# Attention scores of two heads in alternating row halves of TensorE, in a graph layer with mixture of experts

## What is computed

```python
scores = jnp.einsum('hnd,hmd->hnm', q2, k2) * scale + mask[None]
attn = jax.nn.softmax(scores, axis=-1)
out = jnp.einsum('hnm,hmd->hnd', attn, v2)
...
return out @ wo.T + bo
```

## Time and profile before

| | |
|---|---|
| median of 3 runs | 1041.15 us (1040.41 to 1043.7) |
| the profiled execution | 1042.34 us, its span 1040.6 us |
| PE busy | 996.6 us, 96% |
| DVE busy | 775.1 us, 74% |
| ACT busy | 635.5 us, 61% |
| POOL busy | 145.0 us, 14% |
| loop of the heads | about 410 to 540 us of the span |
| score matmuls (L1204) | 144, 64 rows x 128 columns of weights, 384 columns |

### The profile page before, as it was taken

How to read it: one execution, slowest core, us unless ns; L and a number is a source line. 1 busy time by engine, 2 the same in 40 slices (tenths; PEclk the granted TensorE clock), 3 DMA queues, 4 the chain that set the end, 5 groups by cost and what they waited for, 6 DMA issues and landing times.

```text
span 1040.6 us, 15023 instructions
## 1 busy us (share of the span) xinstructions
PE 996.6 (96%) x5191; PEld 848.5 (82%) x5227; DVE 775.1 (74%) x1078; ACT 635.5 (61%) x825; POOL 145.0 (14%) x185
## 2 busy tenths in 40 slices
PE   4999999999999999989999899999999999999898
PEld 4898999888889899978788778788787878788675
DVE  7446888867585869767753788888887878788487
ACT  4357777523322133879952667777777787778472
POOL 3003242410001002243320300000000000000013
PEclk9999999999999999989999899999999999999989
DMA  9562342456546763211105499999999999999886
GB/s 313 168 183 83 100 113 70 126 147 173 166 142 182 213 177 117 82 41 42 41 7 201 182 349 381 386 357 371 378 372 374 374 381 359 363 380 385 298 315 232
DMA packets 140508, 237.33 MB, mean 228 GB/s; under 512 B 6908, under 2 KB 48124, under 8 KB 137892
## 3 DMA queue, kind: packets, MB, share of 16 engines
q1 hardware_dynamic: 135780, 225.91, 63.5%
q0 software_dynamic: 1760, 6.37, 1.6%
q10 hardware_dynamic: 2912, 4.34, 1.1%
HBM read 206.56 MB, written 30.03 MB: 227 GB/s over the span
## 4 chain that ended last, share of the span: by engine, by line
PE 78%; DVE 9%; ACT 7%; DMA 3%; issue 2%; SPq 0%; POOL 0%; ACTq 0%; DVEq 0%; POOLq 0%
PE bank L1322 35%; PE bank L971 5%; PE bank L973 5%; PE bank L972 5%; PE bank L985 4%; PE bank L987 4%; PE bank L986 4%; PE bank L1204 2%; DVE wlo L1397 2%; DMA raw<-in_wffn 2%; PE bank L1121 2%; ACT dense L743 2%; PE bank L1048 2%; PE bank L1218 2%; PE bank L1309 1%
## 5 line engine op out<-in xcount | busy, mean ns | idle before, releaser
L1701 DVE TENSOR_TENSOR wlo<-raw,whi 128x2048 fp32r<-128x2048 f32 x72 | 164.6, 2289 | 28.3 <-ACT whi L869 27.9
L869 ACT ACTIVATE a_all<-raw 128x2048 fp32r<-128x2048 f32 x72 | 138.1, 1918 | 52.5 <-DMA raw<-in_wffn 29.0
L869 ACT ACTIVATE whi<-raw 128x2048 fp32r<-128x2048 f32 x72 | 137.9, 1916 | 42.4 <-DMA raw<-in_wffn 23.5
L1397 DVE TENSOR_TENSOR wlo<-raw,whi 128x1024 fp32r<-128x1024 f32 (+1 forms) x72 | 110.4, 1539 | 49.6 <-ACT whi L658 48.4
L658 ACT ACTIVATE whi<-raw 128x1024 fp32r<-128x1024 f32 (+1 forms) x72 | 89.0, 1242 | 90.8 <-PE bank L973 47.7
L1701 DVE TENSOR_TENSOR t_all<-raw,a_all 128x2048 fp32r<-128x2048 f32 x36 | 82.5, 2293 | 40.8 <-ACT a_all L869 40.6
L971 PE MATMUL bank<-a_all,whi 128*128 128x384 f32 x320 | 109.5, 342 | 0.2 <-DVE t_all L1473 0.2
L1322 PE MATMUL bank<-a_all,xg 128*128 128x512 f32 x360 | 106.7, 410 | 1.0 <-DVE t_all L1701 1.0
L973 PE MATMUL bank<-a_all,wlo 128*128 128x384 f32 x320 | 107.2, 335 | 0.0
L972 PE MATMUL bank<-a_all,whi 128*128 128x384 f32 x320 | 107.1, 335 | 0.0
L1322 PE MATMUL bank<-whi,t_all 128*128 128x512 f32 x288 | 100.4, 410 | 0.0
(11 more groups left out here) (276 smaller groups left out, 2041.5 us busy)
## 6 DMA issues: line engine op xcount, KB each, us to landing
raw<-in_wffn SPq DMA_DIRECT2D x144, 512.0 KB
raw<-in_wffn SPq DMA_DIRECT2D x72, 1024.0 KB
raw<-in_wall SPq DMA_DIRECT2D x28, 1024.0 KB
raw<-in_wall SPq DMA_DIRECT2D x32, 512.0 KB
yrows<-zero SPq DMA_DIRECT2D x24, 512.0 KB, 7.0
y_rows<-zero SPq DMA_DIRECT2D x8, 1024.0 KB, 8.7
dense<-yrows SPq DMA_DIRECT2D x8, 512.0 KB, 7.9
y_rows<-dense ACTq DMA_DIRECT2D x16, 256.0 KB, 5.6
```

What stands on the lines that cost most here:

```text
L869: act.activation(hi_ring[u % RAW], raw[:, u % RAW, :], ACT.Copy).then_inc(hi_done, 2)
L1397: dve.tensor_tensor(ring(wlo, k), part(k), ring(whi, k).bitcast(F32), ALU.subtract).then_inc(lo_done, width(k))
L1701: dve.tensor_tensor(lo_ring[u % RAW], raw[:, u % RAW, :], hi_ring[u % RAW].bitcast(F32), ALU.subtract)\
```

## The change

Scores of both heads of a chunk are made together. A chunk has six tiles, numbered i = 2t + (head in the chunk): the even step makes i = 0 to 3 (row tiles 0 and 1 of both heads), the odd step i = 4 and 5 (row tile 2 of both). The matmuls of a pair alternate between partitions 0 to 63 and 64 to 127. Four banks hold scores, `bank[0:4]`; `bank[3]` was one of the two projection banks. So PE waits in step 0 until all four earlier pieces of the projection have left their banks, and from then on every filling product goes to `bank[7]` and waits for the emptying of the one before.

The odd head's first two tiles are ready a step early, the third tile of both heads in the odd step. So there are three probability buffers instead of two (the third in a part of `mo` that is free by then), PE turns row tiles 0 and 1 of both target tiles first and row tile 2 after a wait of its own. DVE empties the filling product first in its step; in odd steps it normalises ahead of the residuals of the transposed tiles, in even steps behind them as before. Of a chunk's six tiles DVE scales i = 0, 1, 4 and ACT i = 2, 3, 5 (before: two and four). In odd steps ACT has its exponentials ahead of `split2_hi`, in even steps at the old place.

The diff, cut to its core (indented less; the emptyings' new bank index and the statistics' columns are left out in part):

```diff
+prob += [moT[:, KT // 2:KT // 2 + NT, :]]
...
-sc_bank = bank[0:3]
+sc_bank = bank[0:4]
...
 proj_bank = [bank[3], bank[7]]
+TILES = 2 * NT
+def sc_tiles(h):
+    return [(2 * (h // 2) + i % 2, i // 2, i) for i in (range(4, TILES) if h % 2 else range(4))]
+def stat(h, kind, i):
+    return 64 + 20 * (h // 2 % 2) + 6 * kind + i
...
-        if j >= 2:
+        if j >= FIRST2:
+            eng.wait_ge(evicted, 4 * KT + j)
+        elif j >= 2:
             eng.wait_ge(evicted, 4 * KT + j - 1)
...
-        return proj_bank[j % 2]
+        return proj_bank[j % 2 if j < FIRST2 else 1]
...
+    def exps(h):
+        c = h // 2
+        for g, t, i in sc_tiles(h):
+            act.wait_ge(sc_done, TILES * c + i + 1)
+            m, u = stat(h, 0, i), stat(h, 1, i)
+            act.activation(prob[g % 3][:, t, :], prob[g % 3][:, t, :], ACT.Exp, scale=-1.0,
+                           bias=small[:, m:m + 1], accum_out=small[:, u:u + 1]).then_inc(exp_done, 1)
...
+        if h < H and h % 2:
+            exps(h)
         if h % 2 == 1 and (h + 1) // 2 < KT:
             split2_hi((h + 1) // 2)
...
+        if h < H and h % 2 == 0:
+            exps(h)
...
-            for t in range(1, NT):
...
-            last.then_inc(prob_act, 1)
+            for g, t, i in sc_tiles(h):
+                if i in (2, 3, 5):
+                    v = stat(h, 2, i)
+                    act.activation(prob[g % 3][:, t, :], prob[g % 3][:, t, :], ACT.Copy, scale=small[:, v:v + 1]).then_inc(prob_act, 1)
...
-            if i >= 2:
-                pe.wait_ge(mixo_added, i - 1)
+            if i >= 1:
+                pe.wait_ge(mixo_added, i)
             else:
                 pe.wait_ge(evicted, 5 * KT)
             pe.wait_ge(mo_lo, 2)
-        ins = wide(OUT + 2 * j, t, proj_bank[i % 2], *mo_s[kh], True, True, range(2 * half, 2 * half + 2))
+        ins = wide(OUT + 2 * j, t, proj_bank[1], *mo_s[kh], True, True, range(2 * half, 2 * half + 2))
...
+            pe.wait_ge(sc_done, NT * H)
             for t in range(NT - 1):
-                pe.wait_ge(sc_done, NT * (H - 1) + t + 1)
...
         if h < H:
-            lo = HD * (h % 2)
-            q, kk = (qk2[lo:lo + HD, m] for m in range(2))
-            pe.wait_ge(qk_lo, 2 * KT + 2 * (h // 2) + 2)
...
-                    pe.wait_ge(sc_done, NT * (h - 1) + t + 1)
+            c = h // 2
+            pe.wait_ge(qk_lo, 2 * KT + 2 * c + 2)
+            if h == 0:
+                pe.wait_ge(evicted, 4 * KT + FIRST2)
+            tiles = sc_tiles(h)
+            for pair in (tiles[j:j + 2] for j in range(0, len(tiles), 2)):
+                i = pair[1][2]
+                if h % 2:
+                    pe.wait_ge(sc_done, TILES * c + 2)
+                elif c >= 1:
+                    pe.wait_ge(sc_done, TILES * c if i == 1 else TILES * (c - 1) + 4)
                 for n, (q_part, k_part) in enumerate(((0, 0), (0, 1), (1, 0))):
-                    last = pe.matmul(sc_bank[t][:, 0:N], q[:, q_part, t * P:(t + 1) * P], kk[:, k_part, :],
-                                     start=(n == 0), stop=(n == 2))
-                last.then_inc(sc_full, 1)
+                    for g, t, i in pair:
+                        r = slice(HD * (g % 2), HD * (g % 2) + HD)
+                        last = pe.matmul(sc_bank[i % 4][:, 0:N], qk2[r, 0, q_part, t * P:(t + 1) * P], qk2[r, 1, k_part, :],
+                                         start=(n == 0), stop=(n == 2))
+                        if n == 2:
+                            last.then_inc(sc_full, 1)
...
-            pe.wait_ge(prob_ready, g + 1)
-            pe.wait_ge(prob_act, g + 1)
-            for mt in range(NT):
-                if mt == NT - 1:
-                    fill(h, 1)
-                    pe.wait_ge(pt_lo, NT * g + 1)
-                for t in range(NT):
-                    last = pe.transpose(pt_bank[mt][:, t * P:(t + 1) * P], prob[g % 2][:, t, mt * P:(mt + 1) * P], ident[:, :])
-                last.then_inc(pt_full, 1)
+            c = g // 2
+            pe.wait_ge(prob_ready, NT * c + 1 + g % 2)
+            pe.wait_ge(prob_act, NT * c + (3 if g % 2 else 1))
+            def turn(mt, tiles):
+                for t in tiles:
+                    last = pe.transpose(pt_bank[mt][:, t * P:(t + 1) * P], prob[g % 3][:, t, mt * P:(mt + 1) * P], ident[:, :])
+                return last
+            for mt in range(NT - 1):
+                turn(mt, range(NT - 1))
+            pe.wait_ge(prob_ready, NT * c + (2 if g % 2 else 3))
+            for mt in range(NT - 1):
+                turn(mt, (NT - 1,)).then_inc(pt_full, 1)
+            fill(h, 1)
+            pe.wait_ge(pt_lo, NT * g + 1)
+            turn(NT - 1, range(NT)).then_inc(pt_full, 1)
...
+    def minima(h, tiles):
+        c = h // 2
+        for g, t, i in tiles:
+            dve.wait_ge(sc_full, TILES * c + i + 1)
...
+            m = stat(h, 0, i)
+            dve.tensor_tensor_reduce(out=prob[g % 3][:, t, :], in0=sc_bank[i % 4][:, 0:N], in1=mask8[:, t, :],
+                                     scale=-SCALE, scalar=3e38, op0=ALU.add, op1=ALU.min,
+                                     accum_out=small[:, m:m + 1]).then_inc(sc_done, 1)
+    def normalise(h):
+        c, first, n = h // 2, 4 * (h % 2), 2 if h % 2 else 4
+        u, v = stat(h, 1, first), stat(h, 2, first)
+        dve.wait_ge(exp_done, TILES * c + first + n)
+        dve.reciprocal(small[:, v:v + n], small[:, u:u + n]).then_inc(inv_ready, 1)
+        dve.wait_ge(inv_ready, h + 1)
+        for g, t, i in sc_tiles(h):
+            if i in (0, 1, 4):
+                v = stat(h, 2, i)
+                dve.tensor_scalar(prob[g % 3][:, t, :], prob[g % 3][:, t, :], small[:, v:v + 1], None, ALU.mult).then_inc(prob_ready, 1)
...
         if 1 <= h <= KT - FIRST2:
             evict2(K2 + FIRST2 + h - 1)
...
-            dve.tensor_tensor(r, proj_bank[i % 2][:, :], r, ALU.add).then_inc(mixo_added, 1)
+            dve.tensor_tensor(r, proj_bank[1][:, :], r, ALU.add).then_inc(mixo_added, 1)
+        tiles = sc_tiles(h) if h < H else []
+        minima(h, tiles[:len(tiles) // 2])
+        if h >= 2:
+            low_p(h - 2, NT - 1)
+        minima(h, tiles[len(tiles) // 2:])
+        if h < H and h % 2:
+            normalise(h)
         for n in ahead(fill_start[h]) if h in fill_start else ():
             lo(n)
         if 1 <= h <= H:
             for t in range(NT - 1):
                 low_p(h - 1, t)
-        if h < H:
-            dve.wait_ge(exp_done, NT * h + NT)
-            dve.reciprocal(small[:, s + 12:s + 12 + NT], small[:, s + 4:s + 4 + NT]).then_inc(inv_ready, 1)
-            dve.wait_ge(inv_ready, h + 1)
-            dve.tensor_scalar(prob[h % 2][:, 0, :], prob[h % 2][:, 0, :], small[:, s + 12:s + 13], None, ALU.mult).then_inc(prob_ready, 1)
+        if h < H and h % 2 == 0:
+            normalise(h)
```

More of the change, by code:

```diff
@@ L854, in _ @@
                     act.wait_ge(inv_ready, h + 1)
-                    for t in range(1, NT):
-                        i = 76 + 16 * (h % 2) + t
-                        last = act.activation(prob[h % 2][:, t, :], prob[h % 2][:, t, :], ACT.Copy, scale=small[:, i:i + 1])
-                    last.then_inc(prob_act, 1)
+                    for g, t, i in sc_tiles(h):
+                        if i in (2, 3, 5):
+                            v = stat(h, 2, i)
+                            act.activation(prob[g % 3][:, t, :], prob[g % 3][:, t, :], ACT.Copy, scale=small[:, v:v + 1]).then_inc(prob_act, 1)
             def x2_copy(c):
@@ L1657, in low_p @@
                 dve.tensor_tensor(probT[:, 1, t, :], pt_bank[t][:, 0:N], probT[:, 0, t, :].bitcast(F32), ALU.subtract).then_inc(pt_lo, 1)
-            for h in range(H + 2):
-                s = 64 + 16 * (h % 2)
-                for t in range(NT):
-                    if t == NT - 1 and h >= 2:
-                        low_p(h - 2, NT - 1)
-                    if h < H:
-                        dve.wait_ge(sc_full, NT * h + t + 1)
-                        dve.tensor_tensor_reduce(out=prob[h % 2][:, t, :], in0=sc_bank[t][:, 0:N], in1=mask8[:, t, :],
-                                                 scale=-SCALE, scalar=3e38, op0=ALU.add, op1=ALU.min,
-                                                 accum_out=small[:, s + t:s + t + 1]).then_inc(sc_done, 1)
+            def minima(h, tiles):
+                c = h // 2
+                for g, t, i in tiles:
+                    dve.wait_ge(sc_full, TILES * c + i + 1)
+                    if g == 2 and t == 0:
+                        dve.wait_ge(mo_lo, 1)
+                    m = stat(h, 0, i)
[12 more added lines that the diff above has]
+                        dve.tensor_scalar(prob[g % 3][:, t, :], prob[g % 3][:, t, :], small[:, v:v + 1], None, ALU.mult).then_inc(prob_ready, 1)
+            for h in range(H + 2):
                 if 1 <= h <= KT - FIRST2:
```

2 lines of the change are left out of this document (removed).

## The result

| | time, median (lowest to highest) | profiled execution | its span | mean clock of it |
|---|---|---|---|---|
| before | 1040.56 us (1038.77 to 1043.7) | 1042.34 | 1040.6 | 0.988 |
| after | 1048.75 us (1045.6 to 1055.87) | 1055.87 | 1054.1 | 0.977 |

Seven runs of each. The ratio is 1.0084, with an interval of 1.0063 to 1.0105: the change makes the kernel 0.84% slower. The forecast was 1051. Where the two differ is itself a finding.

What follows compares the result with a forecast made beforehand. It took PE as the bound by a small margin over ACT. Entry 2.1, its clock fall 2.1, steps 6 to 15 2.8, step 11's clock fall 2.6 and steps 16 and 17 0.2 made +9.8: 1051 us, range 1041 to 1056.

Steps and rivals of the forecast that it cites:

- Part 1: Score blocks: 1.24 us in even steps, 0.65 in odd, instead of 1.79 each; 13.5 us saved if nothing else were late.
- Part 2: Odd steps 5 to 16: PE stalls 1.3 us before the filling product for DVE's addition; pair 13.3 against 13.6.
- Part 3: Weight halves staged in steps 8, 11, 14: +1.2, +3.1, +1.2 us; steps 6 to 15 +2.8 in sum.
- Part 4: Loop entry: PE waits 3.8 us for the fourth score bank's emptying; +2.1 us by step 6.
- Part 5: PE's clock falls to half after the stands at the entry, +2.1 us, and in step 11, +2.6.
- (a): Rival, loop: quantities of work bind, not orders; odd stand under 0.3 us, time about 1037; chance 0.12.
- A: Theory: waits follow DVE and ACT queue order, clock falls vary; 1034 to 1037 for e8, 1035 to 1037 for e12.
- (b): Rival, loop: waits as forecast, clock falls once or not at all; 1045.5 to 1048.5 us; chance 0.27.
- (c): The forecast itself: both stands, entry and step 11, and both clock falls; 1049 to 1052 us; chance 0.38.
- (d): Rival: POOL's operand split is late in odd steps, next scores wait up to 1 us; 1053 to 1058; chance 0.15.
- (e): Rival: alternating row halves doesn't pay, score products stay at 0.199 us, even blocks 2.4; about 1059; chance 0.03.
- (f): Rival: the stand in odd steps is about half the forecast; 1041 to 1045 us; chance 0.05.

Runs made afterwards that it cites:

- e2: The changed kernel with DVE's addition of the mix tile moved earlier, behind the residuals in the step of its product: 1044.93 us, ratio 1.0049.
- e10: The changed kernel with all score products taken from partitions 0 to 63, one row half: 1060.66 us, ratio 1.0195.
- a2: A second profiled execution of the same changed kernel, nothing altered: 1048.66 us, span 1046.9.
- e3: The changed kernel with three score banks and two projection banks as before, the pairing kept: 1054.99 us, ratio 1.0141.
- e6: The changed kernel with the weight half of step 11 rounded and subtracted in step 12 instead: 1044.7 us, ratio 1.0051.
- e8: The changed kernel with e1, e2 and e6 together, POOL's mix residual earlier in step 4, odd head's first tile scaled in the odd step: 1041.01 us.
- e12: e8 with step 5's weight half staged in step 6, DVE normalising earlier in step 0, projection bank emptied after the normalisation in step 1: 1038.76 us.
- e1: The changed kernel with step 0's projection piece in the attention product's bank, first scores waiting for only three of four emptyings: 1049.39 us.
- e5: The changed kernel with 22 matmuls without use put into PE's stand at the loop entry: 1053.37 us, ratio 1.0137.
- e4: The changed kernel with score matmuls not alternated: three of one head, then three of the other: 1049.1 us, ratio 1.0096.
- e11: The changed kernel with unused matmuls in PE's stands: six per odd step from 7 on, 15 before step 11's last transposes: 1054.69 us, ratio 1.0118.

## Why the prediction was right, by its steps

**Part 1, the pairing.** Even block 1.25 us (forecast 1.24). Odd block 0.73 (466.06 to the next matmul, in e2, where no stand follows), forecast 0.65: slightly too small. e10 shows that the overlap is worth having: without it the changed kernel is 11 us slower.

**Part 2, the odd stand.** Forecast 1.3, measured 1.29 to 1.46, released by the addition, as said. Even step 6.24 to 6.33 (6.26), odd step 7.08 to 7.30 (7.0), pair 13.42 in a2 (13.3). The walk through DVE's queue held within 0.2 for the stand and 0.3 for the step. What I did not say is that the bank is exchangeable: with DVE's queue as late as this, two banks (e3) or an earlier addition (e2) move most of the wait to the attention product.

**Part 3, the weight halves.** Step 11: stand 2.91; in a2 the step takes 10.28, 3.1 more than step 7, forecast +3.1. Steps 8 and 14: stand 0.80, where I had 1.0, and the step 1.0 longer than step 6, where I had 1.2. Steps 6 to 15 in a2, with no fall of the clock: 72.4 against 72.0.

**Part 4, the entry.** Stand 3.94, forecast 3.8; steps 4 and 5 +0.6 to +0.8, forecast +0.6. Step 4 comes 2.6 later (a2) and 3.7 later (after), forecast 3.6 with the clock. The working calls 432.18 to 440.35 step 2; by the earlier trace rows it is step 3. Nothing hangs on it: step 2, from 424.01 in the kernel before, takes 8.17 as well.

**Part 5, the clock**, is the mis-sized term. I took two falls, at the entry and in step 11, +4.7, in every execution. The entry's came in both profiles, step 11's only in after, and after had two more, at stands of 1.40 and 1.46, for which I had planned none. So the number of falls is no property of the kernel alone but differs from execution to execution. Over the runs of the changed kernel the mean clock is 0.984 to 0.989 with one at 0.977, and the time 1045.6 to 1051.7 with that one at 1055.87; the kernel before has 0.988 to 0.993. The middles, 0.987 and 0.990, make about 0.003 x 1050 = 3 us. That is an estimate, and it leaves 5 to 6 of the 8 to 9 us for the waits, for which I had 5.1 (9.8 - 4.7). The profile of a2 says the same of the loop: its +6.5 holds one stretch at half rate more than before, from 414.7 to about 418, worth at most 1.7, which leaves 4.8, where the forecast without the clock was 4.9. The forecast of 1051 was 2 high: 1.6 by the difference to the kernel before (9.8 against 8.2), which the overpriced clock covers, and 0.6 because that kernel's median came to 1040.56, not 1041.15. One reading behind this term was off too: by the 0.63 of the earlier trace rows the fall came 1.2 after 448.02, not 1.5.

**The rivals.** (a) is refuted for the changed kernel by its own sign: the stand before fill A is 1.29 to 1.46, not under 0.3. Its wider form, theory G, that no order helps because ACT and DVE have too much to do, is not settled. It failed in e6 (unchanged at 1049 expected, 1044.7 measured), and e8 shows that orders account for the whole loss. But the gain that A promised from them came in neither e8 nor e12, and there G's bounds, 1040 and 1039, fit better than A's. The Trainium skill, TensorEngine Tiling (Array Packing), section Performance Considerations, says that the emptying of PSUM may become the bottleneck after a 4x speedup of TensorE; the scores here are sped up 1.8x. The runs agree in part: in e3 PE waits 0.73 for a score bank, and in the changed kernel 1.3 to 1.5 for the projection bank, both to be emptied; but moving that one addition in DVE's queue, with no less work, takes the second wait away (e2; one of 0.49 comes up elsewhere). The prediction has DVE and ACT both empty the score tiles; it is DVE alone, by the minimum, and ACT's exponentials take the result from there. (b), one fall only, is what a2 shows, with 1048.66 just above its range of 1045.5 to 1048.5; the median of 1048.75 lies between (b) and (c). (d): in after and a2 no even step waits for POOL's split. (e): refuted by the 1.25. (f): the stands are whole, not half.

## What to carry to other kernels

When PE's work in a step shrinks, follow the next engine's queue operation by operation and ask which of them now stands ahead of the one that PE needs; removing one shared bank only shows the next wait. Heavy rounding and its residual belong into the steps where least waits behind them (2.1 us for one moved half). And look first at waits that are there already: 2.54 us for a residual that POOL could have begun 4.4 us earlier gave 5 us (1041.03 to 1035.96), part of it because the half rate after the wait went too. That is more than a rewrite of the scores gave in any order tried.

## What the runs showed of the hardware

Products over 64 rows overlap when they lie in different row halves: 12 take 1.26 us alternating, 1.26 in groups of three of each half, and 2.28 all in one half. The Trainium skill, TensorEngine Tiling (Array Packing), section Overview, has up to 2x for 64 rows; here it is 2.28 / 1.26 = 1.8. How long a group of one half may be was not tried.

The same stand may or may not bring the clock to its lower level: in step 9 a stand of 1.40 did so in after and the same 1.40 did not in a2, and with the 1.46 of step 15 it was the same. The stand of 2.9 to 3.0 in step 11 came with a fall in five of the eight profiles that have it (after, e1, e3, e5 and e10, not a2, e2 and e4), the stand of 3.9 at the entry in all seven (after, a2, e2, e4, e6, e10, e11).

Matmuls without a use, put into the stand at the entry, kept the clock full there (e5), where it fell in every profile with the bare stand. In e5 and e11 what follows the loop became 2 to 5 us longer (446.3 and 449.0 us against 444.3), although no such matmul stands in it. No run here says why.
